# The first 96 gathers of a tower kernel: groups of four with a wait for the landing, in place of pairs with a memset

## The reference

```python
e = stack([tbl_f[ids[:, f]] for f in range(40)], axis=1)          # 2048 x 40 x 32
z = einsum('bpd,pde,bpe->bp', e[:, iidx], bilinear, e[:, jidx])   # 780 pairs
h = concatenate([z, dense_ctx], axis=1)                           # 2048 x 796
h = relu(h @ W_top1 + b_top1)                                     # 512
h = relu(h @ W_top2 + b_top2)                                     # 256
y = h @ W_top3
```

## Time and profile before

| | |
|---|---|
| median of 3 runs | 728.96 us (727.70 to 730.28) |
| the profiled execution's own time | 728.67 us |
| its span | 726.9 us |
| granted TensorE clock, mean | 0.998 |
| TensorE matmuls, busy | 693.9 us (95% of the span) |
| VectorE, busy | 597.1 us (82%) |
| GpSimd, busy | 522.2 us (72%), 631 instructions |
| ScalarE, busy | 197.1 us (27%) |
| DMA | 22.77 MB, of which 6.84 MB in 13312 packets of the software queue (the gathers) |

### The profile page before, as it was taken

How to read it: one execution, slowest core, us unless ns; L and a number is a source line. 1 busy time by engine, 2 the same in 40 slices (tenths; PEclk the granted TensorE clock), 3 DMA queues, 4 the chain that set the end, 5 groups by cost and what they waited for, 6 DMA issues and landing times.

```text
span 726.9 us, 15700 instructions
## 1 busy us (share of the span) xinstructions
PE 693.9 (95%) x6512; PEld 215.8 (30%) x6512; DVE 597.1 (82%) x608; ACT 197.1 (27%) x309; POOL 522.2 (72%) x631
## 2 busy tenths in 40 slices
PE   2767999999999999999999999999999999999998
PEld 2233333332332232322332232322332222222232
DVE  7989999999986989979876998979967878787800
ACT  3344411422052113043142103143143012213102
POOL 7888888888887888888887888888888887830000
PEclk9999999999999999999999999999999999999999
DMA  4555351222004020000004020000001000000000
GB/s 126 111 89 86 60 99 40 58 52 43 12 12 71 12 40 13 11 12 13 12 12 71 12 35 18 11 12 12 12 12 16 12 12 12 12 8 1 1 1 1
DMA packets 62692, 22.77 MB, mean 31 GB/s; under 512 B 46287, under 2 KB 61805, under 8 KB 62621
## 3 DMA queue, kind: packets, MB, share of 16 engines
q1 hardware_dynamic: 49277, 14.86, 8.8%
q0 software_dynamic: 13312, 6.84, 8.2%
q10 hardware_dynamic: 32, 0.07, 0.1%
HBM read 21.65 MB, written 0.07 MB: 30 GB/s over the span
## 4 chain that ended last, share of the span: by engine, by line
PE 89%; DVE 5%; ACT 4%; DMA 1%; issue 1%; ACTq 0%; DVEq 0%
PE U L940 28%; PE bank_z L965 26%; PE misc L992 14%; PE misc L891 10%; PE U L992 4%; PE U L949 3%; DVE ones L792 3%; PE U L914 3%; ACT x_T L645 1%; DMA idx_wide<-idx_rows 1%; DVE prod L828 1%; ACT x_twin L663 1%; PE bank_z L973 0%; DVE tabs L779 0%; ACT x_twin L666 0%
## 5 line engine op out<-in xcount | busy, mean ns | idle before, releaser
L589 POOL DMA_INDIRECT rows<-in_tbl,idx x416 | 410.2, 986 | 121.3 <-issue 63.5
L828 DVE TENSOR_TENSOR prod<-U,x_T 128x1024 f32<-128x1024 f32 x280 | 329.5, 1216 | 56.5 <-PE U L940 53.7
L965 PE MATMUL bank_z<-prod,select 128*32 128x512 f32 x1600 | 213.1, 604 | 0.7 <-ACT z L625 0.7
L940 PE MATMUL U<-x_T,W 32*128 32x512 f32 x1184 | 187.0, 640 | 7.4 <-ACT x_T L636 3.6
L792 DVE TENSOR_SCALAR ones<-idx_wide,row_of 125x2048 bf16<-125x2048 f16 x140 | 119.0, 872 | 7.0 <-ACT idx_wide L691 3.4
L891 PE MATMUL misc<-ones,tabs 125*32 125x512 bf16 x1680 | 108.4, 388 | 7.3 <-DVE ones L792 5.3
L597 POOL MEMSET pause<- 128x448 uint8 x208 | 111.7, 537 | 0.1
L828 DVE TENSOR_TENSOR prod<-U,x_look 128x1024 f32<-128x1024 f32 x80 | 94.3, 1218 | 21.0 <-PE U L940 18.5
L992 PE MATMUL misc<-z,W 128*32 128x512 f32 x728 | 92.0, 592 | 0.0
L940 PEld LDWEIGHTS U<-x_T,W 32*128 32x128 f32 x1184 | 57.8, 183 | 102.9 <-issue 49.4
L636 ACT ACTIVATE x_T<-U 32x512 f32<-32x512 f32 (+2 forms) x48 | 28.3, 591 | 188.8 <-PE U L914 115.0
(11 more groups left out here) (67 smaller groups left out, 284.1 us busy)
## 6 DMA issues: line engine op xcount, KB each, us to landing
rows<-in_tbl,idx POOLq DMA_INDIRECT x416
idx_wide<-idx_rows SPq DMA_DIRECT2D x13, 500.0 KB
W<-in_W_top SPq DMA_DIRECT2D x100, 8.0 KB
W<-_L_rec_bilinear_matrices SPq DMA_DIRECT2D x72, 16.0 KB, 3.2
prod<-in_tbl SPq DMA_DIRECT2D x4, 156.2 KB
W<-in_W_top SPq DMA_DIRECT2D x35, 2.0 KB
W<-_L_rec_bilinear_matrices SPq DMA_DIRECT2D x4, 128.0 KB
W<-in_W_top SPq DMA_DIRECT2D x1, 512.0 KB
```

Source lines behind the costliest of these rows:

```text
L589: nc.gpsimd.indirect_dma_start(out=rows[:, n % R_SLOTS, t, f, :], out_offset=None, in_=tables[field][:, :], in_offset=bass.IndirectOffsetO ...
L828: last = nc.vector.tensor_tensor(to[:, :, m * N:(m + n) * N].rearrange("p r (m n) -> p r m n", m=n), U[:, at:at + 2, m * N:(m + n) * N].re ...
L940: last = nc.tensor.matmul(U[:, at + r % 2, m * N:(m + 1) * N], W[row, at_W:at_W + P], x_of(o, a)[row, :], start=True, stop=True, skip_grou ...
L965: last = nc.tensor.matmul(bank_z[r * DIM:(r + 1) * DIM, 0:N], sel, prod[:, (2 * g + r // 2) % P_SLOTS, r % 2, m * N:(m + 1) * N], start=(k ...
```

## The change

The first 96 gathers, all those of block 0, lose the memset and its wait after every second gather. After every fourth of them GpSimd waits instead until that gather has landed (`gathered` of its slot at 16 times the gathers begun there). From gather 97 on all is as it was.

```diff
 BURST = 2
+HELD, HELD_BURST = 96, 4
...
                         begun[n % R_SLOTS] += 1
-                        if sum(begun) % BURST == 0:
+                        if sum(begun) <= HELD:
+                            if sum(begun) % HELD_BURST == 0:
+                                pool.wait_ge(gathered[n % R_SLOTS], 16 * begun[n % R_SLOTS])
+                        elif sum(begun) % BURST == 0:
                             pauses += 1
                             nc.gpsimd.memset(pause[:], 0).then_inc(paused, 1)
                             pool.wait_ge(paused, pauses)
```

## The result

The changed kernel takes 750.00 us (median of 4 runs, 746.99 to 752.78) against 729.62 us before (the median with one run more than in the table above): a ratio of 1.027, with a 95% interval of 1.024 to 1.029. The profiled execution took 746.99 us, its span is 745.2. The forecast was slower, 740.6 us, in a range up to 750.0; the median is 9.4 us above the forecast, at the very end of the range, and two of the four runs (751.33 and 752.78) lie beyond it.

A forecast was written before the change was run, and what follows sets the result against it. GpSimd's own rate was taken to bound the kernel. Its delay of 12.5 + 8.5 = 21 us, less 9.1 us free at turn 35, left 11.9 us on the profile's 728.67 us: 740.6 us, range 730 to 750 us.

The forecast's parts named there:

- The bound: GpSimd runs at its own rate up to the last gather; despite 28% idle it never gets lost time back.
- The free delay at the last turn: At turn 35, GpSimd may be 9.1 us late (10.8 us lead less 1.66) before TensorE waits.
- Third and fourth gather at the price of a second: In each group of four, a third gather follows a second after the same 0.30 us gap.
- a held third gather: Rival: the third gather of each four waits 0.76 us, not 0.30; 11 us more in all, 752 us; chance 0.08.
- L in a quiet stretch: Time from the fourth gather's record end to GpSimd's next start, without much load traffic: 1.66 us; break-even is 1.32.
- L while the loads run: The same time from fourth record's end to next start in block 0: 2.96 us beside loads, 1.84 us later.
- its 21: GpSimd's forecast delay in us when block 0's gathers end: 12.5 from the early groups and 8.5 from the later ones.
- the busy stretch: The start of block 0 beside SyncE's loads, taken to end near 66 us and to hold 7.6 groups.
- The end is set by GpSimd's total alone: TensorE's waits in block 0, some 3 us, add nothing to the end; only GpSimd's whole delay at turn 35 counts.
- Quick landings: Rival: the wait after each four stays 1.66 us throughout; 8 us in all, under the 9.1 free; 729 us; chance 0.13.
- Longer landings: Rival: the wait after each four is 4.46 us in the early stretch; 31 us delay, 751 us; chance 0.04.
- The faster rival: First loads land sooner with fewer gathers in flight, giving at most some 2 us plus 0.8 on VectorE; chance 0.04.

The follow-up runs named there:

- e2: Changed kernel with its 24 landing waits moved to gathers 97 to 192, the first 96 in pairs with a memset: 736.08 us, 1.007 of the kernel before.
- e5: Changed kernel with the first 96 gathers in pairs, each with a landing wait, 48 waits in place of 24: 791.96 us in one run.
- e6: Changed kernel with fours and landing waits for gathers 1 to 40 only, then pairs with a memset: 736.28 us, 1.008 of the kernel before.
- e11: Changed kernel with one 500 KB load of index rows moved behind the W_top1 loads: 743.97 us in one run.
- e1: Changed kernel with a memset in place of the landing wait after every fourth of the first 96 gathers: 729.17 us, 0.997 of the kernel before.
- e10: Changed kernel with its landing waits moved to the last 96 gathers, pairs with a memset before them: 731.80 us, 1.001 of the kernel before.
- e4: Changed kernel with no memsets in the 320 gathers after the first 96: 741.26 us, 1.014 of the kernel before.
- e8: Changed kernel with all memsets and landing waits taken out, gathers back to back: 721.40 us, 0.987 of the kernel before.
- e9: Kernel before with its 208 memsets cut from 448 to 8 bytes a partition: 721.83 us, 0.988 of the kernel before.
- e3: Changed kernel with each wait after four gathers set on the landing of the turn before, not the gather just issued: 725.33 us, 0.992 of the kernel before.

## Why the prediction was right, and where its sizes were off

**The bound: right.** GpSimd's rate, with no idle time to spare behind its 28%, was the thing to see. All landing waits of block 0 went into the delay, none was taken up; 4.4 of the 32.1 us came back later, through shorter gathers and memsets.

**The free delay at the last turn: right.** Forecast 10.8 - 1.66 = 9.1 us. Measured: 27.7 us of delay and 18.4 of shift, 9.3 free, and 8.8 to 9.3 in the profiles of e2, e5, e6 and e11.

**Third and fourth gather at the price of a second: right**, by the gaps of 0.30 us and by e1. The rival of a held third gather is out.

**L in a quiet stretch: right.** 1.66 us forecast; ordinary stops are 1.6 to 1.8 and e10's mean is 1.73. The Trainium skill's page "DMA: Bandwidth & Descriptors", section "Anatomy of one DMA — SWDGE (gpsimd) path", gives about 2.0 us for such a DMA and bytes over 436 GB/s on top. The estimate from it, 2.04 us and so an L of 1.36, is too short for this kernel even in the quiet stretch (1.6 to 1.8 us), and more so beside the loads (up to 6.03).

**L while the loads run: the term that was mis-sized.** Forecast 7.6 stops of 2.96 and 16.4 of 1.84, 52.7 us. Measured: seven stops up to 69 us with a mean of 3.64 (4.79, 2.88, 4.72, 1.77, 2.06, 3.26, 6.03), and 62.2 us in all, 2.59 each. That is 9.5 of the 11.1 us by which the delay at gather 97 missed its 21. Another 1.4 us are the longer gathers (1045 against 1031 ns, 96 times). About half of the 9.5 us lies in the first seven stops. The other half lies in the seventeen after 69 us, 2.16 us each against the 1.84 forecast: stops of 2.60, 3.43, 5.55 and 2.68 us stand between 86 and 169 us, so the busy stretch does not end near 66 us as the sum took it. Two parts of the reading were at fault as well. I counted packets until they reached 32 for each gather, but in the kernel before later gathers are in flight, and their packets can fill the count while one of the earlier gather is still missing. So it was a lower bound, and I used it as a value; how much that took off was not measured. And I took 0.46 us from the last packet to the restart everywhere; it is 0.56 at gather 96, but 1.1 at gather 28, and 1.6 at gather 68 (last packet 4.0 us after its record). The size of one load's share is shown by e11; part of the miss is chance, as the same 24 stops sum to 62.2, 73.3 (e4) and, with the load moved, 59.2 us (e11); which part of the remaining early stops belongs to which load was not tried.

**"The end is set by GpSimd's total alone": it fits the number here, and is wrong as a rule.** The prediction let the waits in block 0 pass because they don't add to the end. Here they did not add: the end moved by the 18.4 us of GpSimd's total, not by 13.2 more. But the total is only the larger of the two, and e4, which repairs it, keeps the shift of block 0. I had noted a wait of some 3 us at turn 8. It became a shift of 13.2, in waits before turns 4, 5, 7 and 8, since the delay there was 31 us and not 21. The 12 us of waits that I expected before turns 32 to 35 were 4.6. With a larger lead at the end the same change would still have cost about 13 us, by e4.

**The sum with measured terms.** 27.7 - 9.3 = 18.4 us, and 745.2 - 726.9 = 18.3 in the spans. The medians are 20.4 us apart; runs of the changed kernel spread over 5.8 us, runs before over 3.8, and only one execution of each was read step by step. That the median is still inside the range is luck: the delay at gather 97 was half as large again as forecast (32.1 us against 21), and only the fastest execution, the profiled one at 746.99, is accounted for by this sum.

**The rivals.** Quick landings are out in block 0 and true in block 3 (e10). Longer landings, the rival at 751 us, is nearest in time, though not all stops were that long: its mean of 4.46 was reached by three of the first seven. The faster rival asked for more room for the first loads; the first turns do come about 1 us earlier (turn 2 at 51.10 against 52.13 us in the same view), but one-hots are 752 ns in the first 60 us against 847, and in e8, which has neither stops nor memsets, turn 2 stands at 49.35. So it is the missing memsets that give it, not more room for the loads. I had priced that with the median, 753 against a least of 733. The mean, 847, is what counts on a chain, and e8 and e9 show that it was worth 7 to 10 us over the whole kernel (7.8 and 7.3 in the spans, 9.7 and 9.4 in the medians).

## What to carry to other kernels

An engine that shows 28% idle may still have nothing to give: look at what each gap is, and measure its slack as the lead of its results over their use, at the end of each block as well as at the last use. A wait for a transfer just issued costs the whole landing, here 1.7 us in quiet and up to 6 beside bulk loads; a wait for one a group older cost nothing (e3). Counting packets in a shared queue gives a lower bound for a landing, not its time.

## What had not been expected

A memset on GpSimd of 448 bytes a partition, 0.54 us long and of no use but as a pause, lengthened VectorE's one-hot instructions (2048 columns, bf16 from f16) from 769 to 886 ns on average. Shortened to 8 bytes (155 ns) or taken out, it made the kernel 1.2 to 1.3% faster than before: 721.83 us (0.988, 0.985 to 0.992) and 721.40 us (0.987, 0.984 to 0.989). The gathers beside the one-hots hardly do this: in e8 GpSimd issues them back to back and the one-hots stay at 767 ns on average, 745 in the median. e3 and e1, which have 48 and 24 of the 208 memsets less, point the same way (0.992 and 0.997). e8 and e9 are the best versions found, and neither needs a pause for speed. The Trainium skill states in "SBUF — State Buffer", section "Who interferes with whom", that some VectorE instructions use a pair of memory ports that GpSimd uses too, and that whichever issues first has the pair for its whole instruction while the other is fully blocked. The trace of the kernel before agrees: where memset and one-hot overlap, one of them ends a fixed time after the other, 549 to 552 ns (40 times) or 403 to 406 ns (22 times), as if it had started only then. That it is this pair of ports no run here shows.
